# First layer's two edge layers in row tiles and quadrants of TensorE, with one PSUM bank moved from the sums to them

## The reference, cut to what matters

```
h = gelu(edge_attr_8 @ Wfc1 / sqrt(8))      # 8 -> 64
h = gelu(h @ Wfc2 / sqrt(64))               # 64 -> 64
w = h @ Wfc3 / sqrt(64)                     # 64 -> 192
gs, gv = f_s[src], f_v[src]
mid0 = w0 * gs * y0
mid1 = w3 * sum(gv * y1) / sqrt(3)
mid2 = (w1 * gs) * y1
mid3 = w2 * gv * y0
ns0, ns1, nv2, nv3 = segment sums of mid0..mid3 over dst / sqrt(32)
```

## Time and profile before

| | us |
|---|---|
| median of 3 runs | 3056.2 |
| lowest, highest | 3023.99, 3060.04 |
| the profiled execution, whole | 3079.29 |
| its span, first to last instruction | 3077.1 |
| mean granted TensorE clock | 0.795 |

### The profile page before, as it was taken

One profiled execution on the slowest core, in us unless ns is written; L12 is line 12 of the kernel. 1 busy time (PEld: TensorE's weight loads), 2 busy tenths in 40 slices (PEclk: granted clock), 3 DMA queues, 4 the chain that ended last, 5 costly groups with the idle time before them and its releaser, 6 DMA issues.

```text
span 3077.1 us, 77590 instructions
## 1 busy us (share of the span) xinstructions
PE 2732.5 (89%) x24164; PEld 2006.0 (65%) x24164; DVE 1638.9 (53%) x4537; ACT 972.3 (32%) x2395; POOL 2004.7 (65%) x1630
## 2 busy tenths in 40 slices
PE   8768777887788888888899999999999999999996
PEld 4334434444444444444588888888888888888983
DVE  3446333443443443433466666666666666666664
ACT  2212212121121211121244444444444444444442
POOL 4555554554555555555188888888888888888884
PEclk5565666556655556665599999999999999999998
DMA  6233332232332332333278888888888887888887
GB/s 191 60 94 92 83 85 76 81 94 77 82 85 78 86 89 80 87 88 81 76 141 140 141 139 140 140 140 140 141 140 141 141 139 140 140 142 143 142 137 176
DMA packets 386447, 354.44 MB, mean 115 GB/s; under 512 B 60080, under 2 KB 337136, under 8 KB 386064
## 3 DMA queue, kind: packets, MB, share of 16 engines
q0 software_dynamic: 150528, 141.40, 31.9%
q1 hardware_dynamic: 231248, 206.49, 24.0%
q10 hardware_dynamic: 4544, 4.93, 0.6%
HBM read 244.83 MB, written 133.44 MB: 123 GB/s over the span
## 4 chain that ended last, share of the span: by engine, by line
PE 75%; another core or an unknown queue 12%; issue 6%; DVE 3%; ACT 2%; SPq 1%; DMA 1%; DVEq 0%; POOL 0%; ACTq 0%; POOLq 0%
PE ps_o L1043 11%; PE ps_w L1031 10%; PE ps_d L1052 8%; PE ps_o L1041 8%; PE ps_x L1065 6%; PE ps_w L894 6%; PE ps_h L887 5%; PE ps_h L882 5%; PE ps_p L838 5%; PE ps_x L1005 3%; PE ps_g L853 2%; PE ps_g L847 1%; PE ps_g L850 1%; PE ps_nd L910 1%
## 5 line engine op out<-in xcount | busy, mean ns | idle before, releaser
L620 POOL DMA_INDIRECT tab<-summed,sidx x784 | 1223.7, 1561 | 285.1 <-issue 229.1
L602 POOL DMA_INDIRECT gat<-f,gidx x784 | 751.8, 959 | 714.3 <-DVE feats L1350 409.6
L1490 DVE TENSOR_TENSOR prod<-ps_w,xg 128x768 f32<-128x768 f32 x392 | 375.5, 958 | 268.6 <-PE ps_w L1031 255.6
L1043 PE MATMUL ps_o<-ro_v,prod 128*128 128x96 f32 x3136 | 479.1, 275 | 0.0
L1043 PEld LDWEIGHTS ps_o<-ro_v,prod 128*128 128x128 f32 x3136 | 414.1, 192 | 0.0
L793 ACT ACTIVATE xg<-ps_x 128x768 f32<-128x768 f32 x392 | 296.4, 808 | 338.2 <-PE ps_x L1065 336.3
L887 PE MATMUL ps_h<-h,w 128*128 128x256 f32 x392 | 225.2, 675 | 178.9 <-issue 106.5
L1031 PE MATMUL ps_w<-hid,wf 64*128 64x128 f32 x4704 | 369.4, 290 | 2.0 <-ACT hid L794 2.0
L1041 PE MATMUL ps_o<-ro_s,prod 96*128 96x96 f32 x1568 | 328.0, 291 | 20.0 <-DVE msg L1501 6.8
L1031 PEld LDWEIGHTS ps_w<-hid,wf 64*128 64x128 f32 x4704 | 294.1, 187 | 70.3 <-issue 44.8
L1052 PE MATMUL ps_d<-msg,same 128*128 128x193 f32 x1568 | 332.3, 334 | 0.7 <-ACT summed L812 0.7
(11 more groups left out here) (259 smaller groups left out, 3330.0 us busy)
## 6 DMA issues: line engine op xcount, KB each, us to landing
xt<-in_src_rows SPq DMA_DIRECT2D x196, 256.0 KB
xt<-feat SPq DMA_DIRECT2D x784, 36.0 KB
xt<-in_ea SPq DMA_DIRECT2D x196, 128.0 KB
feat<-xt SPq DMA_DIRECT2D x25, 576.0 KB
hot_dst<-in_dst_rows SPq DMA_DIRECT2D x98, 128.0 KB
gat<-f,gidx POOLq DMA_INDIRECT x784
hot_dir<-sh_rows SPq DMA_DIRECT2D x98, 128.0 KB
xt<-hot_dst SPq DMA_DIRECT2D x196, 64.0 KB
```

Of the source, the lines that this page charges most:

```text
L602: pool.indirect_dma_start(out=gat[:, r % 4, k, :], out_offset=None, in_=t["f0"], in_offset=bass.IndirectOffsetOnAxis(ap=gidx[:, r // 4, at ...
L620: pool.indirect_dma_start(out=t["tabs"][into[k]], out_offset=bass.IndirectOffsetOnAxis(ap=sidx[:, r, k:k + 1], axis=0), in_=summed[:, r, k ...
L1043: last = pe.matmul(ps_o[:, k, 96 + 64 * c:192 + 64 * c], prod[:, ur % 2, k, 1 + c, :], ro_v[:, c, :], start=True, stop=True)
L1490: dve.tensor_tensor(prod[:, r % 2, :, :, :].rearrange("p k c e -> p k (c e)"), ps_w4[:, :, 0:3 * P], xg[:, r // 2, r % 2 * 2:r % 2 * 2 + 2 ...
```

## The change

`layer1` becomes two matmuls of 128 columns, each with 16 partitions in, at partitions 0 and 32 (two row tiles of the array), one into the bank `ps_h`, one into a new bank `ps_hy`. `layer2` becomes four matmuls of 64 partitions in, 64 out and 128 columns, the four quadrants of the array; the two row halves write different banks. `w1`, `w2` and the layout of the attributes in DRAM follow: the attributes come as 48 partitions of 128 columns, of which 16 are unused zeros, and four more small weight transfers are issued at the start. Each gelu becomes two instructions of 128 columns. `layer3` takes its four tiles in the order 0, 2, 1, 3, which alternates the row halves. To free a bank, tile sums (320 columns) and both window sums (96 columns each) share one bank, `ps_pg`; so `tile_sums` also waits for `acc_done`, that VectorE has added the window sums of the group before.

```diff
-            ea8 = sb(c2, "ea8", [16, 2, 256])
+            ea8 = sb(c2, "ea8", [48, 2, P])
...
             ps_h = pb(c2, "ps_h", [P, 512])
-            ps_h1, ps_h2 = ps_h[:, 0:256], ps_h[:, 256:512]
+            ps_hy = pb(c2, "ps_hy", [P, 512])
+            ps_h1 = [ps_h[:, 0:P], ps_hy[:, 0:P]]
+            ps_h2 = [ps_h[:, P:2 * P], ps_hy[:, P:2 * P]]
...
-            ps_p = pb(c2, "ps_p", [P, 512])
-            ps_gw = pb(c2, "ps_g", [P, 2, 256])
-            ps_g = [ps_gw[:, i, :] for i in range(2)]
+            ps_pg = pb(c2, "ps_pg", [P, 512])
+            ps_p = ps_pg[:, 0:FEAT]
+            ps_g = [ps_pg[:, FEAT + 4 * WIN * i:FEAT + 4 * WIN * (i + 1)] for i in range(2)]
...
-                    act.activation(h1[:, r % 2, :], ps_h1[:, :], ACT.Gelu_apprx_tanh,
-                                   scale=8.0 ** -0.5).then_inc(g1_done, 1)
+                    for q in range(2):
+                        last = act.activation(h1[:, r % 2, P * q:P * q + P], ps_h1[q], ACT.Gelu_apprx_tanh, scale=8.0 ** -0.5)
+                    last.then_inc(g1_done, 1)
...
-                    pe.matmul(ps_h1[:, :], w1[:, :], ea8[:, r, :], start=True, stop=True).then_inc(h1_ready, 1)
+                    for q in range(2):
+                        at = slice(32 * q, 32 * q + 16)
+                        last = pe.matmul(ps_h1[q], w1[at, :], ea8[at, r, :], start=True, stop=True)
+                    last.then_inc(h1_ready, 1)
...
-                    pe.wait_ge(g1_done, u + 1)
                     since(pe, g2_done, u)
-                    pe.matmul(ps_h2[:, :], w2[:, :], h1[:, r, :], start=True, stop=True).then_inc(h2_ready, 1)
+                    settled(pe, g1_done, u + 1, passed)
+                    for c in range(2):
+                        for h in range(2):
+                            rows_h, cols_c = slice(S * h, S * h + S), slice(S * c, S * c + S)
+                            last = pe.matmul(ps_h2[h][cols_c, :], w2[rows_h, cols_c], h1[rows_h, r, P * c:P * c + P],
+                                             start=True, stop=True)
+                    last.then_inc(h2_ready, 1)
...
-                    for k in range(G):
+                    for k in (0, 2, 1, 3):
...
                             since(pe, part_done, u)
+                            since(pe, acc_done, u)
                             pe.wait_ge(sel_ready, u + 1)
```

More of the change, by code:

```diff
@@ L233, in gnn_kernel @@
             c2 = ExitStack()
-            w1 = sb(c2, "w1", [16, P])
+            w1 = sb(c2, "w1", [48, P])
             w2 = sb(c2, "w2", [P, P])
@@ L391, in _ @@
                 for h in range(2):
-                    sp.dma_start(w1[8 * h:8 * h + 8, S * h:S * h + S], t["L0_gnn_Wfc1"]).then_inc(w_in, 16)
-                    sp.dma_start(w2[S * h:S * h + S, S * h:S * h + S], t["L0_gnn_Wfc2"]).then_inc(w_in, 16)
+                    for q in range(2):
+                        sp.dma_start(w1[32 * q + 8 * h:32 * q + 8 * h + 8, S * h:S * h + S], t["L0_gnn_Wfc1"]).then_inc(w_in, 16)
+                    for q in range(2):
+                        sp.dma_start(w2[S * h:S * h + S, S * q:S * q + S], t["L0_gnn_Wfc2"]).then_inc(w_in, 16)
                     sp.dma_start(w3raw[S * h:S * h + S, :], t["L0_gnn_Wfc3"]).then_inc(w_in, 16)
@@ L398, in load_ea8 @@
                     since(sp, h1_ready, u - 1)
-                    sp.dma_start(ea8[:, r, :], t["ea8"][:, bass.ds(u * 256, 256)]).then_inc(ea8_in[r], 16)
+                    sp.dma_start(ea8[:, r, :], t["ea8"][:, bass.ds(u * P, P)]).then_inc(ea8_in[r], 16)
                 def load_rows():
@@ L675, in _ @@
                 act.activation(src_f[:, :], src_i[:, :], ACT.Copy).then_inc(src_set, 1)
-                act.wait_ge(w_in, 16 * 6)
+                act.wait_ge(w_in, 16 * 10)
                 act.activation(w3[:, :], w3raw[:, :], ACT.Copy, scale=1.0 / 8.0).then_inc(w3_ok, 1)
@@ L744, in gelus @@
                     since(act, w_ready, u - 1)
-                    act.activation(h2[:, r % 2, :], ps_h2[:, :], ACT.Gelu_apprx_tanh,
-                                   scale=1.0 / 8.0).then_inc(g2_done, 1)
+                    for h in range(2):
+                        last = act.activation(h2[:, r % 2, P * h:P * h + P], ps_h2[h], ACT.Gelu_apprx_tanh, scale=1.0 / 8.0)
+                    last.then_inc(g2_done, 1)
                     if r % 4 == 0 and runs(u + 4, NGRP):
@@ L875, in _ @@
                 pe.wait_ge(res_ready, NT)
-                pe.wait_ge(w_in, 16 * 6)
+                pe.wait_ge(w_in, 16 * 10)
                 pe.wait_ge(w3_ok, 1)
@@ L1094, in _ @@
                     pe.wait_ge(w_in4, 16 * (8 + 2 * len(WF2_PARTS)))
-                    join(ps_p, 1)
+                    join(ps_pg, 1)
                     hidden(0, 0, 0)
@@ L1678 @@
         "ea3": cols(pad(arr["edge_attr_3"], EP, 1)), "ea4": cols(pad(arr["edge_attr_4"], EP, 0)),
-        "ea8": np.ascontiguousarray(ea8.reshape(NGRP, 2, 256, 8).transpose(1, 3, 0, 2)).reshape(16, NGRP * 256),
+        "ea8": np.zeros((48, NGRP * P), np.float32),
         "ea64": np.ascontiguousarray(ea64.reshape(NGRP, 2, 2, P, 64).transpose(0, 2, 4, 1, 3)).reshape(NGRP, P, 256),
     }
+    halves = ea8.reshape(NGRP, 2, 2, P, 8).transpose(1, 2, 4, 0, 3).reshape(2, 16, NGRP * P)
+    data["ea8"][0:16], data["ea8"][32:48] = halves[0], halves[1]
     for name in arr:
```

## The result

The changed kernel took 3087.3 us (median, 3082.9 to 3091.3), the kernel before on the same chip 3053.8: a ratio of 1.0126, 95% interval 1.0076 to 1.0176. (Ratios leave out runs in a slower state of the chip and are taken over all others of both kernels, so they can differ by a thousandth or two from the quotient of two medians.) The forecast was 2973 us, faster; it is 1.3% slower, clear of the noise but under the 2% that counts as a difference. The profiled executions lie closer together, span 3081.1 against 3077.1, so the traces explain where the expected 83 us went more than where the last 1% came from.

The account below looks back on a forecast made before the run. TensorE's chain at half clock, plus late completions, was taken to bound the first layer. Gains of 0.64 us a step over 0.8 of 196 steps gave 100 us, less a sixth 83: 2973 us from 3056.2; range 2880 to 3100.

Parts of the forecast that it names:

- L882 to row tiles: First edge layer's matmul as two row tiles: 1.15 to 0.72 us at half clock, a gain of 0.43.
- L887 to quadrants: Second edge layer's matmul as four quadrants side by side: 0.72 us at half clock, a gain of 0.43.
- rivals 1 and 3: L887's quadrants: 1, run as pairs, gain nothing, 3031 us, chance 0.15; 3, run one behind the other, 3201 us, 0.08.
- The new wait: Tile sums wait for VectorE's add of the group before: 0.35 us in a quiet step, nearly all of L882's gain.
- a sixth of the gain goes to that: First layer: late completions at half clock take a sixth of the 100 us gain, leaving 83 us.
- the subtraction of 0.7: First layer: TensorE without a stop needs 6.66 us of the 7.37 us step; 0.7 is left, at late completions.
- The same two rows say that a fall of the clock by itself costs nothing here.: First layer: steps take 7.33 us at clock 0.50, the same as at the mean of 0.60; clock priced at nothing.
- Rival 2: Shared bank makes TensorE and VectorE take turns, tile sums wait for late adds: 70 us slower, 3126 us, chance 0.15.
- Rival 4: First layer: late completions vanish if TensorE stays at half clock; step 6.0 us, 265 us shorter, 2791 us, chance 0.10.
- The floor: GpSimd's four gathers a group: no first-layer step below 5.0 us for long; not the bound yet.

Follow-up runs that it names:

- experiment 6: The changed kernel with two idle matmuls of 128 columns a step, behind the tile sums and behind layer two: 3064.0 us, ratio 1.1644, prompt chip.
- experiment 1: The kernel before with only the shared bank and its wait for the add: 2652.9 us against 2635.2, ratio 1.0059, prompt chip.
- before_filled: The kernel before with two idle matmuls of 128 columns a step, no shared bank: ratio 1.0081, again 1.0105, both on late chips.
- experiment 7: Four kernels, late chip: before_filled 1.0081, the covered gap 1.0222, quads_only 1.0069, and the changed kernel with one idle 64-column matmul before the tile sums 1.0119.
- experiment 5: The kernel before with the shared bank and only the first edge layer in two row tiles: 2646.7 us, ratio 1.0049, prompt chip.
- quads_only: The kernel before with the shared bank and the second edge layer in quadrants, the first whole: ratio 1.0069, late chip.
- the covered gap: The changed kernel with two idle matmuls a step, the first moved ahead of the tile sums' wait for the bank: ratio 1.0222, again 1.0291, late chips.

## Why the prediction was wrong

*The direction.* It was wrong: 34 us slower for a forecast of 83 faster. The prediction's last sentence had named this outcome: "It is wrong if TensorE's pieces shrink as said and the step stays at 7.4: then late completions set the step." That is what the trace shows.

*L882 to row tiles.* Right: 0.74 for a forecast of 0.72. *L887 to quadrants.* Right, and better: about 0.63 for 0.72; rivals 1 and 3 fall. The slope by columns, read from rows of other shapes, carried both.

*The new wait.* Right at half clock where no completion is late: 0.36 for 0.35 us, and a quiet step of 5.49 (experiment 6) for 5.50. At full clock, which the prediction left out, it is longer, 0.80 us in the chain of experiment 1. Over the whole layer it is 222.7 us on the late chip, some 1.16 a step, because the add is late itself.

*"Of the steps at half clock some are held by late completions (0.7 us in the mean) and a sixth of the gain goes to that".* This is the step that failed, and with it the subtraction of 0.7 as if it were a delay beside TensorE's work. I charged a sixth, 17 of 100 us; it was all of it. The 87 us of TensorE's time that did fall away came back in full as idle time, most of it in front of the tile sums. Time in which TensorE waits for the others, which themselves wait for its completions, is not a constant added to each step; it grows when TensorE gets ahead.

*"The same two rows say that a fall of the clock by itself costs nothing here."* Right for the time on a late chip (before_filled, clock 0.71, no gain), but I left out what it does to the saving. The two edge layers were to take 0.43 + 0.43 = 0.86 us less of TensorE at half clock. Over the 193 steps between 60 and 1480 us that is 166, which at a mean clock of 0.60 is 166 x 0.5 / 0.60 = 138 us. Measured are 146 by line, so the cost of the pieces was right. But the other matmuls took 54 us more, since more of them ran at half clock, and 87 are left in all. The clock went from 0.60 to 0.56; with quadrants and the bank it is 0.56 too (experiment 7), with the bank alone 0.61, and with the bank and the row tiles it is higher than before (experiment 5, on a prompt chip). So the fall goes with the quadrants; the row tiles alone didn't run on a late chip. Why the quadrants have it no run here shows.

*Rival 2, the shared bank.* Its mechanism is in the trace (the steps from 844.87 on), its price is not: the bank alone is 1.0059 on a prompt chip and 1.0016, same as before, on a late one. The argument against it, that the wait for the add would lie inside time that is lost anyway, held. (By its own sum, 54 late adds against a gain of 61 us, it would have made the kernel slower from 1.1 us each on, not 1.3.) The 1.3% of the change lies beyond the bank's interval on a late chip; the 0.7% of quads_only overlaps it (1.004 against 1.0059). So the splits probably cost a little there; that it is through the lower clock isn't shown, since a higher clock (before_filled) gave no gain.

*Rival 4, late completions go with full clock.* It had 0.10. In the kernel before, completions of the tile sums that fall in stretches at full clock are late by 3.0 us in the median (70 of them) and those at half clock by 0.04 (113), by the semaphore events. But with the share down from 0.19 to 0.12 the step stayed, so late completions didn't vanish with the full clock. The 2791 us were far off.

*The floor.* On a prompt chip the same change meets GpSimd's 5.0 us a step (5.11 measured, before and after), and gains nothing either. Two different bounds, one outcome.

What stays open: what makes TensorE's completions late on some chips (it isn't the fetching of instructions; VectorE's and ScalarE's instructions take the same time on both, L1350 548 and 547 ns), what about the quadrants, and about sixteen passes of 4 columns, keeps TensorE at 1.2 GHz longer, and whether the last per cent is the clock's. Open too is the filled kernel's 16% on a prompt chip: its quiet steps are TensorE at half clock with 0.36 us of waiting, but neither the filled kernel before nor the covered gap ran on such a chip, so whether bank, quadrants or the added work keep the clock down there isn't told apart. No version beat the kernel before.

## What to carry to other kernels

An engine that is busy eight tenths of a stretch isn't the bound because it looks busiest: add up its idle time, look at who releases it, and ask whether those wait for it in turn; then a shorter piece only makes the wait longer. A bank shared between two engines puts a wait into each step, and what it costs depends on what else the engine waits for: 0.6% of the time on a prompt chip, nothing measurable on a late one, where the waits came to 211.7 us in all. A shorter form of a matmul can also change the granted clock and so the price of its neighbours: look at rows that weren't touched (54 us here). And a small wait that recurs in a slow stretch isn't yet its cause: look for a kernel with the same wait and another clock. Before counting on a saved half microsecond, compare the step with the next floor, here GpSimd's 5.0 us, and measure on more than one chip.

## What was not expected of the hardware

- The same kernel takes about 2635 us in two groups of runs and 3051 to 3077 in four others, all of the difference in the first layer (997 against 1437 us), with VectorE's and ScalarE's instructions as long. What differs is when TensorE's semaphore updates come: the window sums' 0.02 and 1.04 us after their modelled end in the median.
- Work added to TensorE changed its clock both ways: two idle matmuls of 128 columns a step raised it from 0.60 to 0.71 in the kernel before and lowered it to 0.50 (late chip) and 0.54 (prompt chip, from 0.79) in the changed one; sixteen passes of 4 columns lowered it to 0.53, and it stood at 0.50 through 14 us without any gap.
- The second edge layer in quadrants goes with a lower clock on both kinds of chips, the row tiles and the shared bank don't: over the whole program 0.775 to 0.786 against 0.803 to 0.817 with bank and quadrants (late chip), on a prompt chip 0.909 to 0.921 with bank and row tiles and 0.880 to 0.895 with the quadrants as well, against 0.899 to 0.912.
- Four quadrants of 64 by 64, two passes each, run side by side: about 0.63 us at half clock for all eight, where the whole 128 by 128 matmul of 256 columns takes 1.15.
